# One-core AdaLN feed-forward kernel: group 0 split around group 1, x sums of groups 2 and 3 moved to VectorE, a new step table and a longer warm-up

## What is computed

```python
q_emb = relu(cond @ W3 + b3)
h0 = relu(((n * x + x.sum(axis=1)) * q_emb[:, None, :]) @ W2 + b2)     # n = 64 tokens
# ternary_weight, in groups of 64: scale = max(mean|w|, 1e-8); w -> clip(round(w / scale), -1, 1) * scale
h  = square(relu(h0 @ ternary_weight(w_fc).T))
hn = h * rsqrt(mean(h * h, axis=-1) + eps)
out = x + hn @ ternary_weight(w_proj).T
```

## Time and profile before

| | us |
|---|---|
| three timed runs | 322.00, 322.94, 325.56 |
| median | 322.94 |
| the profiled execution, its device time | 322.21 |
| its span in the trace | 320.2 |
| PE busy in the span | 312.3 (98%) |

### The profile page before, as it was taken

The page is one execution under the profiler, slowest core; times in us unless marked ns, Lnnn a source line. Parts: engine busy times, 40 slices in busy tenths (PEclk is TensorE's granted clock), DMA queues, the critical chain, the costliest instruction groups (busy, mean ns, idle before and its releaser), DMA issues.

```text
span 320.2 us, 3832 instructions
## 1 busy us (share of the span) xinstructions
PE 312.3 (98%) x1324; PEld 237.8 (74%) x1324; DVE 210.4 (66%) x290; ACT 192.2 (60%) x282; POOL 113.1 (35%) x94
## 2 busy tenths in 40 slices
PE   5999999999999999999999999999999999999995
PEld 5764655544888788888888888888888888888884
DVE  0449989798898856677555665855665675665545
ACT  1659797899996885445554444654445554445550
POOL 1003333234643535414334441334443314443330
PEclk9999999999999999999999999999999999999999
DMA  6994959588411110007000000610000024000003
GB/s 199 299 311 114 282 130 271 142 189 248 119 36 34 33 36 1 0 14 250 0 0 2 0 0 0 215 51 0 0 2 0 0 105 159 0 0 2 0 1 132
DMA packets 31332, 27.02 MB, mean 84 GB/s; under 512 B 18737, under 2 KB 20817, under 8 KB 31313
## 3 DMA queue, kind: packets, MB, share of 16 engines
q1 hardware_dynamic: 29984, 26.25, 29.0%
q10 hardware_dynamic: 1328, 0.53, 0.7%
HBM read 18.39 MB, written 4.19 MB: 71 GB/s over the span
## 4 chain that ended last, share of the span: by engine, by line
PE 89%; ACT 4%; issue 3%; DVE 2%; DMA 1%; DVEq 0%; ACTq 0%
PE ps_out L320 34%; PE ps_acc L307 32%; PE ps_acc L291 17%; PE ps_out L272 4%; ACT x_t L558 1%; ACT x_t L555 1%; DMA h_f<-in_cond_dram 1%; PE ps_acc L367 1%; DVE abs_sum L408 1%; DVE y_hi L448 1%; PE ps_x L372 1%; ACT w_scale L528 0%; ACT w_t L535 0%; ACT w_abs L522 0%; PE ps_x L352 0%
## 5 line engine op out<-in xcount | busy, mean ns | idle before, releaser
L209 POOL TENSOR_TENSOR wv_sb<-wv_sb 128x512 f32<-128x512 f32 x55 | 82.2, 1495 | 114.0 <-ACT wv_sb L561 114.0
L320 PE MATMUL ps_out<-w_t,y_hi 128*128 128x512 f32 x256 | 101.7, 397 | 0.2 <-DVE y_lo L450 0.2
L320 PE MATMUL ps_out<-w_t,y_lo 128*128 128x512 f32 x256 | 101.0, 394 | 0.0
L307 PE MATMUL ps_acc<-h_hi,w_t 128*128 128x512 f32 x256 | 100.1, 391 | 0.0
L307 PE MATMUL ps_acc<-h_lo,w_t 128*128 128x512 f32 x256 | 100.0, 391 | 0.0
L450 DVE TENSOR_TENSOR y_lo<-x_t,y_hi 128x512 fp32r<-128x512 f32 x64 | 91.3, 1427 | 2.2
L555 ACT ACTIVATE x_t<-ps_acc 128x512 f32<-128x512 f32 x64 | 38.1, 595 | 81.1 <-PE ps_acc L307 81.0
L448 DVE CAST y_hi<-x_t 128x512 fp32r<-128x512 f32 x64 | 29.2, 457 | 73.5 <-PE ps_out L320 65.7
L320 PEld LDWEIGHTS ps_out<-w_t,y_hi 128*128 128x128 f32 x256 | 48.1, 188 | 11.6 <-DVE y_lo L450 0.6
L320 PEld LDWEIGHTS ps_out<-w_t,y_lo 128*128 128x128 f32 x256 | 48.3, 189 | 10.9
L307 PEld LDWEIGHTS ps_acc<-h_hi,w_t 128*128 128x128 f32 x256 | 48.3, 189 | 10.6 <-issue 0.2
(11 more groups left out here) (46 smaller groups left out, 144.0 us busy)
## 6 DMA issues: line engine op xcount, KB each, us to landing
x_sb<-in_x_dram SPq DMA_DIRECT2D x7, 1024.0 KB, 5.8
raw<-in_L_ffn_W_fc_dram SPq DMA_DIRECT2D x8, 512.0 KB, 5.9
raw<-in_L_ffn_W_proj_dram SPq DMA_DIRECT2D x8, 512.0 KB, 6.4
out_dram<-x_t SPq DMA_DIRECT2D x16, 256.0 KB, 2.1
x_sb<-in_x_dram SPq DMA_DIRECT2D x4, 256.0 KB, 5.6
wv_sb<-in_L_cond_W_dram SPq DMA_DIRECT2D x4, 256.0 KB, 7.0
x_t<-in_L_cond_W_dram ACTq DMA_DIRECT2D x1, 512.0 KB, 4.3
w_turned<-w_tern SPq DMA_TRANSPOSE x16, 3.1
```

Of the source, the lines that this page charges most:

```text
L209: engine.tensor_tensor(sq_acc[:], sq_acc[:], y_sq[:, v % SQ_RING, :], ALU.add).then_inc(sq_added, 1)
L307: last = pe.matmul(ps_acc[:, (UNITS + v) % ACC_RING, :], w_t[:, j, k * P:(k + 1) * P], part[:, k, g * BANK:(g + 1) * BANK], start=(k == 0 ...
L320: last = pe.matmul(ps_out[:, t, :], part[:, v % RING, t * P:(t + 1) * P], w, start=(j == 0 and part is y_hi), stop=(j == HJ - 1 and part i ...
```

## The change

Five edits.

1. **Order of tiles.** The 64 tiles run in five stretches: tiles j = 0 to 7 of group 0, all of group 1, tiles 8 to 15 of group 0, group 2, group 3. A tile v is looked up in TILE_AT. So weight pairs 8 to 15 are first used from tile 16 on and not from tile 8 on.
2. **Five read-outs of `ps_out`.** After the first stretch DVE copies it aside (`set_aside`, four copies); after the third it adds the rest and then finishes (`merge`, four additions and four multiply-adds). Results are now written into `x_res` in place and stored from there; `load_res` waits for the stores. The squares have two accumulators.
3. **x sums of groups 2 and 3.** PE only transposes (line 308 of the new file); for each k DVE reduces over the batch, forms 64*x + sum, and multiplies with q: three instructions for one. `sum_x(2)` stands ahead of unit 4 and `sum_x(3)` ahead of unit 8, and `scale_x(g + 1, m)` stands in unit 4g + m for g = 1 and 2. Group 1 keeps its place and its form.
4. **Step tables.** Nine steps in the units (twelve before), seven in the tiles (four before).
5. **Start.** `ident_f` is built first with its own semaphore, ten dummy matmuls run before cond is waited for and two after its transposes. The bias load on ACT's queue goes ahead of w_q.

```diff
-WARM_UP = 6
+WARM_UP = 10
...
+    STRETCHES = [(0, 0, HJ // 2), (1, 0, HJ), (0, HJ // 2, HJ), (2, 0, HJ), (3, 0, HJ)]
+    TILE_AT = [(r, g, j) for r, (g, first, end) in enumerate(STRETCHES) for j in range(first, end)]
+    START = [sum(end - first for _, first, end in STRETCHES[:r]) for r in range(len(STRETCHES) + 1)]
...
-    STEP_AT_UNIT = {0: 0, 1: 1, 3: 2, 4: 3, 5: 4, 7: 5, 8: 6, 9: 7, 11: 8, 12: 9, 13: 10, 15: 11}
-    STEP_AT_TILE = {1: 12, 3: 13, 5: 14, 7: 15}
-    KEEP_AT_TILE = {8: 14, 9: 15}
+    STEP_AT_UNIT = {1: 0, 3: 1, 5: 2, 8: 3, 10: 4, 12: 5, 13: 6, 14: 7, 15: 8}
+    STEP_AT_TILE = {0: 9, 3: 10, 6: 11, 9: 12, 12: 13, 14: 14, 16: 15}
+    def sums_by_vector(g):
+        return g > 1
+
+    KEEP_AT_TILE = {17: 14, 18: 15}
...
-            def load_res(g):
-                if g == 0:
+            def load_res(n):
+
+                if n == 0:
                     sp.wait_ge(xt_done, KD * GROUPS)
                 else:
-                    sp.wait_ge(finished, TT * g)
-                sp.dma_start(x_res[:], x_rows[g]).then_inc(res_loaded, 16)
+                    sp.wait_ge(stored, 16 * TT * n)
+                sp.dma_start(x_res[:], x_rows[STRETCHES[n + 1][0]]).then_inc(res_loaded, 16)
...
+                if i == 0:
+                    load_x(2)
                 turn_pair(i)
                 if i == 1:
-                    load_x(2)
-                if i == 4:
                     load_x(3)
-                if i == 9:
+                if i == 6:
                     load_res(0)
...
                 for k in range(KD):
                     for t in range(TT):
-                        last = sum_x_block(t, k)
+                        if sums_by_vector(g):
+                            last = pe.transpose(ps_out[:, k, t * P:(t + 1) * P], x_sb[:, t, k * P:(k + 1) * P], ident_f[:])
+                        else:
+                            last = sum_x_block(t, k)
                     last.then_inc(xt_done, 1)
...
-            pe.wait_ge(consts_ready, 1)
+            pe.wait_ge(ident_ready, 1)
+            for i in range(WARM_UP):
+                pe.matmul(ps_acc[:, 1, 0:P], ident_f[:], ident_f[:], start=True, stop=True)
             pe.wait_ge(cond_loaded, 16)
...
-            for i in range(WARM_UP):
+            for i in range(2):
...
-                if u % KD == SUMS_AT and u // KD + 1 < GROUPS:
+                if u == SUMS_AT:
+                    sum_x(1)
+                if u % KD == 0 and 0 < u // KD < GROUPS - 1:
                     sum_x(u // KD + 1)
                 make_h0(u)
...
-                dve.tensor_tensor(x1, ps_out[:, k, :].rearrange("p (b n) -> p b n", n=N),
+                src = ps_out[:, k, :].rearrange("p (b n) -> p b n", n=N)
+                if sums_by_vector(g):
+                    at = 2 * (KD * (g - 2) + k)
+                    wait(dve, summed, at)
+                    dve.tensor_reduce(batch_sum[:], src, AX.X, ALU.add).then_inc(summed, 1)
+                    dve.wait_ge(summed, at + 1)
+                    dve.scalar_tensor_tensor(out=x1, in0=src, scalar=float(N),
+                                             in1=batch_sum[:].rearrange("p (b o) -> p b o", o=1).to_broadcast([P, GB, N]),
+                                             op0=ALU.mult, op1=ALU.add).then_inc(summed, 1)
+                    dve.wait_ge(summed, at + 2)
+                    src = x1
+                dve.tensor_tensor(x1, src,
...
+            def set_aside():
+
+                for t in range(TT):
+                    dve.wait_ge(tile_summed, t + 1)
+                    dve.tensor_copy(partial[:, t, :], ps_out[:, t, :]).then_inc(finished, 1)
+
+            def merge(r):
+
+                inverse_root(r)
+                for t in range(TT):
+                    dve.wait_ge(finished, t + 1)
+                    dve.wait_ge(tile_summed, TT * r + t + 1)
+                    dve.tensor_tensor(partial[:, t, :], ps_out[:, t, :], partial[:, t, :], ALU.add).then_inc(finished, 1)
+                dve.wait_ge(rstd_ready, r)
+                dve.wait_ge(res_loaded, 16 * r)
+                dve.wait_ge(finished, TT * (r + 1))
+                for t in range(TT):
+                    dve.scalar_tensor_tensor(out=x_res[:, t, :], in0=partial[:, t, :], scalar=rstd[:, t:t + 1],
+                                             in1=x_res[:, t, :], op0=ALU.mult, op1=ALU.add).then_inc(merged, 1)
...
-                if g + 1 < GROUPS and m == SUMS_AT:
+                if u == SUMS_AT:
                     for k in range(KD):
-                        scale_x(g + 1, k)
+                        scale_x(1, k)
+                if 0 < g < GROUPS - 1:
+                    scale_x(g + 1, m)
...
+            act.dma_start(bq_t[:], b_q.rearrange("(m p) -> p m", p=P), allow_slow_non_contiguous=True).then_inc(bias_loaded, 16)
             act.dma_start(wq_sb[:], w_q.rearrange("(k p) d -> p k d", p=P)).then_inc(wq_loaded, 16)
-            act.dma_start(bq_t[:], b_q.rearrange("(m p) -> p m", p=P), allow_slow_non_contiguous=True).then_inc(bias_loaded, 16)
```

More of the change, by code:

```diff
@@ L208, in add_squares @@
                 engine.wait_ge(sq_added, v)
-                engine.tensor_tensor(sq_acc[:], sq_acc[:], y_sq[:, v % SQ_RING, :], ALU.add).then_inc(sq_added, 1)
+                engine.tensor_tensor(acc, acc, y_sq[:, v % SQ_RING, :], ALU.add).then_inc(sq_added, 1)
         @block.sync
@@ L312, in project_tile @@
             def project_tile(v, t):
-                g, j = v // HJ, v % HJ
+                r, g, j = TILE_AT[v]
                 c, i = j // TT, j % TT
                 w = w_t[:, HJ + KD * c:HJ + KD * (c + 1), i * P:(i + 1) * P]
-                if j == 0:
-                    wait(pe, finished, TT * (g - 1) + t + 1)
+                if opens(v):
+                    wait(pe, finished, TT * (r - 1) + t + 1)
                 for part in (y_hi, y_lo):
                     last = pe.matmul(ps_out[:, t, :], part[:, v % RING, t * P:(t + 1) * P], w,
-                                     start=(j == 0 and part is y_hi), stop=(j == HJ - 1 and part is y_lo))
-                if j == HJ - 1:
+                                     start=(opens(v) and part is y_hi), stop=(closes(v) and part is y_lo))
+                if closes(v):
                     last.then_inc(tile_summed, 1)
@@ L389, in _ @@
                 hidden(v + AHEAD)
[L390 to L391 removed]
+                r = TILE_AT[v][0]
+                if closes(v) and r > 0:
+                    sum_squares(r)
                 project(v)
@@ new lines, in finish, with read_out @@
+            def finish(r):
+                inverse_root(r)
+                dve.wait_ge(rstd_ready, r)
+                dve.wait_ge(res_loaded, 16 * r)
+                for t in range(TT):
+                    dve.wait_ge(tile_summed, TT * r + t + 1)
+                    dve.scalar_tensor_tensor(out=x_res[:, t, :], in0=ps_out[:, t, :], scalar=rstd[:, t:t + 1],
+                                             in1=x_res[:, t, :], op0=ALU.mult, op1=ALU.add).then_inc(finished, 1)
+            def read_out(r):
+                if r == 0:
+                    set_aside()
+                elif STRETCHES[r][0] == 0:
+                    merge(r)
+                else:
+                    finish(r)
@@ L503, in _ @@
             for v in range(TILES):
-                if v % HJ == AHEAD - 1 and v >= HJ:
-                    inverse_root(v // HJ - 1)
-                    finish(v // HJ - 1)
+                r = TILE_AT[v][0]
+                if r > 0 and v == START[r] + AHEAD - 1:
+                    read_out(r - 1)
                 if v == TILES - 2:
@@ L509, in _ @@
                 split_y(v)
-                if v % HJ == HJ - 1 and v < TILES - 1:
-                    sum_parts(v // HJ)
+                if closes(v) and 0 < r < GROUPS:
+                    sum_parts(r)
                 if v in STEP_AT_TILE:
                     step(STEP_AT_TILE[v])
-            inverse_root(GROUPS - 1)
-            finish(GROUPS - 1)
+            read_out(GROUPS)
         @block.scalar
```

120 lines of the change are left out of this document (64 added, 56 removed).

## The result

The changed kernel takes 327.18 us (median of 8 executions, 326.47 to 329.0), the kernel before 324.31 in the same rounds (8, 321.59 to 325.56). The ratio of the two is 1.013, with a 95% interval of 1.009 to 1.017: slower by 1.3%, clear of the noise. The profiled execution took 329.0, with a span of 327.2, against 322.21 and 320.2.

What follows compares the result with a forecast made beforehand. PE's own work, busy for 98% of the span, was taken to bound the kernel. Gains of 4.2 and losses of 5.7 us made net +1.5, so 322.2 + 1.5 = 323.7 us, range 319.0 to 327.0.

Steps and rivals of the forecast that it cites:

- Term 5: Extra read-outs, set_aside and merge: a loss of 0.1 and of 0.8 us (0 to 4.0 for merge).
- Term 2: Start of the kernel: a gain of 0.4 us (-0.3 to +1.2), and the old wait of 0.2 goes.
- Term 1: Sums of groups 2 and 3: sixteen transposes take 1.8 us instead of 3.57, a gain of 3.6 (0 to 4.0).
- Rival D: Sums of groups 2 and 3: the transposes are no cheaper than the matmuls, 326.2 us; chance 0.08.
- Term 3: Second sums: DVE's scalings take 2.05 us each, so PE waits 1.1 us (0 to 2.8) ahead of them.
- Rival C: Second sums: DVE's new scaling runs slower beside POOL, 3.05 us each, 329.3 in all; chance 0.12.
- Term 4: Units 12 to 15 and tile 0: ACT falls behind with its steps, PE loses 3.7 us (2 to 5).
- Rival B: The stalls don't come, 0.9 left of 5.7 us of losses, 318.9 in all; chance 0.22.
- Rival E: Second sums: PE falls to 1.2 GHz after transposes and a wait, 326.7 us; chance 0.06.
- A: The main case, the sum of all terms: 323.7 us, 321 to 326 by their ends; chance 0.52.

Runs made afterwards that it cites:

- before_start: The kernel before with the new start alone (ident_f first, ten dummies ahead of cond, two behind, bias load first): 323.09 us, ratio 0.9991 to the kernel before.
- merge_late: The changed kernel with the four multiply-adds of merge moved behind the split of tile 34: 325.22 us, ratio 1.003 to the kernel before.
- before_pad: The kernel before with an unused buffer of 32 bytes a partition (batch_sum) ahead of abs_sum: ratio 1.000 to the kernel before.
- all_four: The changed kernel with batch_sum last, merge's multiply-adds behind split_y of tile 34, step 2 in unit 4, steps 7 to 15 later: 319.45 us, ratio 0.9885.
- steps_later: The changed kernel with steps 7 to 15 later, unit 14 without a step, last copies at tiles 19 and 20: 324.2 us, ratio 1.0034 to the kernel before.

## Why the prediction was wrong

The sum gave 323.7, and the changed kernel took 327.2 in its median, without the lower clock. Of the 3.5 between them Term 5 is 1.1 (1.9 and not 0.8), the pace of hidden, which had no term, 1.4, and Term 2 is 0.6. Each of the other terms is right within two tenths.

**Term 1 held.** Sixteen transposes took 1.75 and 1.94 us against 1.8, so 0.109 and 0.121 us a record, near the 0.112 that I took from the records of the sums. Rival D fell: one record takes the place of two at the same pace. Whether it is the load of the weights that sets this pace was not tried.

**Term 2 failed by 0.6 in its place, and in its base.** The dummies ran at 0.232 us a record for all twenty, where I had counted on some at 0.112, so q began at 7.6 and not at 6.7. More important, I took one execution at the fast end of 321.6 to 325.6 as the base and left its start at that. The same start has another length in other executions, and the long warm-up takes that away, a gain that is not in the sum. It would explain why the medians are only 2.9 apart where the profiled executions differ by 4.9 without the lower clock. before_start was to show it and didn't, so this is argued only.

**Term 3 held**, on DVE of the changed kernel in order of time, one scaling with the rounding that follows:

```profile
42.84 0.68 DVE L477 TENSOR_REDUCE batch_sum<-ps_out 128x8 f32<-128x512 f32 x1
43.55 0.69 DVE L479 SCALAR_TENSOR_TENSOR x_t<-ps_out,batch_sum 128x512 f32<-128x512 f32 x1
44.28 0.69 DVE L484 TENSOR_TENSOR x_t<-x_t,q_t 128x512 f32<-128x512 f32 x1
44.89 0.42 DVE L491 CAST h_hi<-h_f 128x512 fp32r<-128x512 f32 x1
```

From 42.84 to 44.89 are the 2.05 of the prediction, and the second transposes start at 47.50, 16.7 after the first, where the sum gave 16.55 and a start. Rival C, a scaling held by POOL, didn't come; step_unit4, which takes the step out of unit 5, has no such wait.

**Term 4 held to a tenth**: relu(15) stood at 18.5 after unit 12's start at 63.2, and this is ACT of the changed kernel at that place:

```profile
81.10 0.68 ACT L629 ACTIVATE h_f<-ps_acc,bv_t 128x512 f32<-128x512 f32 x1
81.67 0.59 ACT L634 ACTIVATE x_t<-ps_acc 128x512 f32<-128x512 f32 x1
...
83.49 1.04 ACT L614 ACTIVATE w_t<-w_turned 128x1024 fp32r<-128x1024 bf16 x1
```

Its relu is done at 81.78, 18.6 after; project(1) came at 26.6, as forecast. Rival B, that the stalls don't come, fell. steps_apart takes steps out of this stretch and the three waits go, so the steps are their cause.

**Term 5 failed: "four more from SBUF, at 0.62 to 0.65".** It was mis-sized at 0.8 and measured 1.8 to 1.9. The additions ended as I said. The first three multiply-adds take 0.75 each and 0.66 from start to start (206.1 to 208.1), which is near the forecast; the last is held to 1.78 by POOL. I had the row that tells it, and wrote it down as a behaviour, but put no price of 1.0 on it; with it the term is 1.8. No run takes POOL's addition away from beside the multiply-add, so that POOL holds it is read from the rows: once in the changed kernel, once more in merge_late. The Trainium skill, "SBUF — State Buffer", section "SBUF: two separate sides", says that a DVE operation with two SBUF inputs and a GpSimd operation take their shared ports in turn, the later one blocked for the whole of the other; the trace agrees, with 1.78 beside POOL's addition and 0.75 three times without.

**Rival E came, at another place and without its transposes.** I looked for the lower clock at the second transposes, and behind them the first layer kept its pace: 6.88 us for 16 records at 49.44, where the kernel before takes 13.74 for 32. It came behind the merge's wait, in three of eight executions, for 1.9 us. A wait that Term 5 had at 0.8 was no place to look for it.

**There was no term for what only moves addresses.** A new buffer of 32 bytes cost 1.4 us, without a wait or an instruction more: after_end, with the buffer at the end, has hidden at 1.82 again. The prediction took over "hidden takes 1.82 to 1.85" from the kernel before and gave a change of pace no term and no reason for leaving it out. The diff showed the buffer; that it would cost anything, the profile of before could not show.

**One of the chances doesn't add up.** C, half of D and half of E are 0.19 without anything of A; for slower I wrote 0.17.

## What to carry to other kernels

Lay the engines' rows end to end through a seam: that gave two stalls to a tenth of a microsecond. Then price every row that shows two durations for one instruction, and look at what runs beside the new ones. Compare the mean of the most frequent instruction before and after, and if it moved with no wait, try where the buffers lie; and look at how the executions of the kernel before scatter before one of them is made the base.

## What the runs showed of the hardware

- The pace of PE's matmuls of hidden and project depends on where the small buffers with `y_hi` and `y_lo` lie, and hidden doesn't read these: 3.681, 3.708, 3.660 and 3.680 us for the two halves of a tile at 0, 32, 64 and 96 bytes. The same page of the Trainium skill, in the same section, says that PE's port never waits on another engine. As I read it, no address of buffers that it doesn't read should then matter to hidden, and the measurement differs. Whether DVE's writes or ACT's and POOL's reads beside it are behind this was not tried.
- 1.82 us without a matmul, in the middle of a kernel in which PE is otherwise busy, was followed, after 1.1 us at full pace, by 3.5 us at the 1.2 GHz level, in some executions and not in others. The waits of 1.27, 0.83 and 1.03 in the first tiles were not, in the profile of the changed kernel.
- The granted clock reads 1.00 while twenty dummies run at 0.232 us a record in the changed kernel, and while q takes 3.25 us in before_pad in place of 1.99. The rate of the records tells the level there, the column doesn't.
- Transposing DMAs landed after 3.1 us in the median of sixteen, and the last but one after 4.75 us in all_four and 4.70 in steps_later; in every profile one of them took 6.2 us or more.
